# A graph-attention layer on one Trainium2 core: the second round in another order, the pair products as one row, a shared normalise, and a new load order

## The chip, the cores and the metric

The kernel runs on one core of one Trainium2 chip. Five engines work side by side: TensorE (PE, matrix products, weight loads as PEld), VectorE (DVE), ScalarE (ACT), GpSimd (POOL) and SyncE (SP, which here only issues DMAs). Each works through its own list of instructions in order, and waits at semaphores for the others. The metric is the device time of one execution in microseconds, lower is better; the median of several runs counts.

## What is computed

The input x has 128 graphs of 64 nodes with 384 features, and adj is a 128 x 64 x 64 matrix of integer edge types. Cut to what matters, the reference is:

```python
h = jnp.maximum(_layernorm(x, axis=-1), 0.0)
dep_emb = dep_emb_table[adj]
hi_t = einsum('bid,de->bie', h, W1_w[:HID])[:, :, None, :] + einsum('bijd,de->bije', dep_emb, W1_w[HID:]) + W1_b
hj_t = einsum('bjd,de->bje', h, W2_w[:HID])[:, None, :, :] + einsum('bijd,de->bije', dep_emb, W2_w[HID:]) + W2_b
relevance = jnp.sum(hi_t * hj_t, axis=-1)
A = softmax(where(adj != 0, relevance, NEG), axis=2)
h_syn = relu(einsum('bij,bjd->bid', A, h) @ gcn_w + gcn_b)
out = x + h_syn @ Wo_w + Wo_b
```

adj holds only 0 and 1 here, so every edge has the same embedding. With p and q the two projections of that embedding, the relevance becomes h M h^T plus a term per row, a term per column and a constant, with M = W1 W2^T and the "pair products" W2 p, W1 q and p.q.

## The kernel before

The 128 graphs are cut into 16 rounds ("supers", NSUP = 16, LAST = 15) of 8 graphs, that is 512 rows of x, as four tiles (k) of 128 rows. The features are three chunks (c, d) of 128. Every large product is made in float16 with a high and a low part of each operand, three matmuls for one (`split_product`, L1028 to L1030: high x high, high x low, low x high). For each round s:

- **h** is the normalised input. VectorE makes the statistics (L637), POOL makes ln_mul and ln_add in 20 small dependent steps (`coefficients`, L340), ScalarE writes h_tok (float32) and the high half of h_parts (float16) with two passes for each tile (`normalise`, L451), POOL subtracts to get the low half (`token_low`, L402), and a DMA transposes h_parts into one of two buffers hT (L261). Rounds 0 and 1 are transposed by TensorE instead (`early_transposes`, L1073).
- **G = M h^T** in three chunks (`g_chunk`) into PSUM banks 0 to 2. ScalarE writes the high half and a whole copy (L483, L488), VectorE the low half (`g_low_part`, L785).
- **hg = h gcn_w** in four tiles (`hg_tile`) into banks 0, 1, 2 and 0 again, so each tile waits until G's bank has been read (`g_split`). A 385th column is the row term of the scores. ScalarE copies the high half (L502), VectorE the row term and the low half (L908, L712). SP moves the halves into hg_parts by DMA (`move_hg`).
- **scores** (L1106), softmax on VectorE and ScalarE (L915 to L951, L611), attention transposed on TensorE (L1222), copied by ScalarE (L573) and VectorE (`attention_high`, L889), then **aggregation** z = A hg one round later (L1255, L1260), z's halves by ScalarE (`z_parts`, L495, L497) and VectorE (`z_low_part`, L894), and the output product with Wo (`O_BANK`), added to x by VectorE (L902). POOL adds the bias Wo_b to x before (`add_bias`, L408).

The order is written out by hand for each engine. TensorE's round s is: G(s) with the transposed attention of round s-1 inside it, hg tile 0, aggregation of s-1, hg tiles 1 to 3, scores(s), output(s-1). The first two rounds stand apart. The **head** loads W1 and W2, transposes them, makes M and the pair products, makes power-of-two scales for gcn_w and M out of their peaks (`peak_to_row`, `row_top`, `peak_to_all`: column to row on TensorE, maximum on VectorE, one value to all partitions on TensorE), and computes hg(0) (banks 0, 1, 2, 4), G(0) and scores(0). The **second round** is `iteration(1, prev2=False)` of each engine: G(1), hg tiles 0 and 1 with the attention's transpose between them, aggregation, hg tiles 2 and 3, scores, output. A branch on has_types (`typed`, L244) stands before the transposes of round 1; it is taken only for adjacencies with more than one type, and its condition is computed by VectorE (L794, `types_known`).

## Time and profile before

| | |
|---|---|
| median of 3 runs | 378.81 us (375.56 to 379.2) |
| the profiled execution's own time | 379.19 us |
| its span, first to last instruction | 377.3 us |
| mean granted TensorE clock | 0.982 |
| TensorE busy | 358.4 us, 95% |
| TensorE weight loads | 222.8 us, 59% |
| VectorE busy | 268.2 us, 71% |
| ScalarE busy | 273.7 us, 73% |
| GpSimd busy | 178.3 us, 47% |
| share of TensorE in the chain that ended last | 87% |

The profile is one execution. Its timeline gives for every engine the start of an instruction, its length and, in brackets, how long the engine stood idle before it and what released it. The windows view gives for a stretch how long each engine was busy and the mean granted clock of TensorE (1.00 is 2.4 GHz, 0.50 is 1.2 GHz). Matmuls overlap: a row's length is longer than the distance to the next one.

### The profile page before, as it was taken

Reading aid. Unit: us, or ns where it says so; the run is one execution under the profiler, and the core shown is the slowest. Engines: PE = TensorE matmul, PEld = TensorE weight load, DVE = VectorE, ACT = ScalarE, POOL = GpSimd, SP = SyncE. Lnnn points to the kernel's source line nnn. Section 1 sums busy time; section 2 is a strip of 40 time slices with the busy share of each in tenths; the row PEclk is TensorE's granted clock in tenths of the full one; section 3 lists DMA queues with packets and bytes.
Section 4 is the critical chain, followed back from the end, with each engine's and each line's share of the span. In section 5 each row is a group of like instructions: output and inputs, shape, how many; then the busy total and the mean of one; then the engine's idle time right before and its main releaser. Section 6 shows DMA issues by size and latency. Waiting matters only on the chain.

```text
span 377.3 us, 9541 instructions
## 1 busy us (share of the span) xinstructions
PE 358.4 (95%) x3154; PEld 222.8 (59%) x3154; DVE 268.2 (71%) x665; ACT 273.7 (73%) x580; POOL 178.3 (47%) x349
## 2 busy tenths in 40 slices
PE   7899883999999999999999999999999999999986
PEld 6564542656575656656565757566665656575653
DVE  1688878659686877777694958677776859576674
ACT  2375679297969788787879697887878787964733
POOL 2017506647372728274655637282836565490000
PEclk9889998799999999999999999999999999999999
DMA  8972412439564839384654646393937543434043
GB/s 237 287 246 80 108 65 50 119 104 171 151 164 130 203 83 250 84 220 114 187 126 133 156 140 175 97 236 83 250 83 199 135 127 78 132 87 147 19 123 130
DMA packets 82215, 53.87 MB, mean 143 GB/s; under 512 B 45666, under 2 KB 82148, under 8 KB 82196
## 3 DMA queue, kind: packets, MB, share of 16 engines
q1 hardware_dynamic: 81492, 52.64, 51.7%
q10 hardware_dynamic: 640, 0.79, 0.7%
q0 software_dynamic: 64, 0.20, 0.3%
q8 instruction: 11, 0.18, 0.2%
q14 instruction: 8, 0.07, 0.1%
HBM read 17.44 MB, written 12.58 MB: 80 GB/s over the span
## 4 chain that ended last, share of the span: by engine, by line
PE 87%; DVE 5%; ACT 4%; DMA 2%; issue 1%; ACTq 0%; DVEq 0%
PE bank L1028 23%; PE bank L1029 23%; PE bank L1030 23%; PE bank L1106 6%; PE bank L1260 3%; PE bank L1255 3%; PE bank L1080 2%; DMA e_col<-L_gnn_dep_emb_table_dram 2%; PE bank L1222 1%; ACT bank L611 1%; ACT h_parts L451 1%; ACT h_tok L460 1%; PE bank L1323 1%; ACT h_tok L451 1%; PE bank L1325 1%
## 5 line engine op out<-in xcount | busy, mean ns | idle before, releaser
L402 POOL TENSOR_TENSOR h_parts<-h_tok,h_parts 128x1536 f16<-128x1536 f32 x14 | 43.4, 3098 | 99.0 <-ACT h_parts L451 99.0
L1028 PE MATMUL bank<-gw_hi,hT 128*128 128x385 f16 (+2 forms) x204 | 65.2, 324 | 7.6 <-DVE hg_lo L712 6.1
L1030 PE MATMUL bank<-gw_hi,hT 128*128 128x385 f16 (+2 forms) x204 | 64.9, 323 | 0.0
L1029 PE MATMUL bank<-gw_lo,hT 128*128 128x385 f16 (+2 forms) x204 | 64.8, 322 | 0.0
L1028 PE MATMUL bank<-wo_hi,z_hi 128*128 128x384 f16 x180 | 58.7, 326 | 0.0
L1029 PE MATMUL bank<-wo_lo,z_hi 128*128 128x384 f16 x180 | 58.7, 326 | 0.0
L1030 PE MATMUL bank<-wo_hi,z_lo 128*128 128x384 f16 x180 | 58.7, 326 | 0.0
L408 POOL TENSOR_TENSOR x_all<-x_all,bo_all 128x1536 f32 (+1 forms) x16 | 56.2, 3520 | 0.0
L1028 PE MATMUL bank<-hT,m_hi 128*128 128x512 f16 x144 | 54.6, 379 | 0.0
L1030 PE MATMUL bank<-hT,m_lo 128*128 128x512 f16 x144 | 54.6, 379 | 0.0
L1029 PE MATMUL bank<-hT,m_hi 128*128 128x512 f16 x144 | 54.6, 379 | 0.0
L785 DVE TENSOR_TENSOR g_parts<-bank,g_parts 128x512 f16<-128x512 f32 x48 | 33.0, 690 | 23.9 <-ACT bank L488 23.5
L483 ACT ACTIVATE g_parts<-bank,pair_bias 128x512 f16<-128x512 f32 x48 | 32.9, 686 | 15.9 <-PE bank L1030 15.8
L451 ACT ACTIVATE h_tok<-x_all,ln_add,ln_mul 128x384 f32 (+1 forms) x56 | 39.3, 702 | 5.7 <-POOL ln_add L340 5.7
L495 ACT ACTIVATE z_hi<-bank,gcn_bias 128x512 f16<-128x512 f32 x48 | 33.7, 702 | 11.8 <-PE bank L1260 11.8
L502 ACT ACTIVATE hg_hi<-bank 128x384 f16<-128x384 f32 x64 | 32.5, 509 | 13.0 <-PE bank L1030 13.0
L451 ACT ACTIVATE h_parts<-x_all,ln_add,ln_mul 128x384 f16 (+1 forms) x56 | 39.1, 698 | 0.0
L894 DVE TENSOR_TENSOR z_lo<-bank,z_hi 128x512 f16<-128x512 f32 x48 | 32.8, 683 | 8.5 <-ACT bank L497 8.5
L902 DVE SCALAR_TENSOR_TENSOR x_all<-bank,out_scale,x_all 128x384 f32 (+1 forms) x64 | 36.4, 610 | 1.5 <-PE bank L1329 1.1
L712 DVE SCALAR_TENSOR_TENSOR hg_lo<-bank,hg_hi 128x384 f16<-128x384 f32 x64 | 35.0, 550 | 0.2 <-issue 0.2
L497 ACT ACTIVATE bank<-bank,gcn_bias 128x512 f32<-128x512 f32 x48 | 32.6, 678 | 0.0
L1028 PEld LDWEIGHTS bank<-gw_hi,hT 128*128 128x128 f16 x204 | 20.0, 99 | 21.3 <-DVE hg_lo L712 6.5
(149 smaller groups left out, 679.7 us busy)
## 6 DMA issues: line engine op xcount, KB each, us to landing
x_all<-in_x_dram SPq DMA_DIRECT2D x16, 768.0 KB, 6.4
out_dram<-x_all SPq DMA_DIRECT2D x15, 768.0 KB, 4.0
hg_parts<-hg_lo SPq DMA_DIRECT2D x32, 192.0 KB, 3.0
hg_parts<-hg_hi SPq DMA_DIRECT2D x32, 192.0 KB, 3.2
out_dram<-x_all SPq DMA_DIRECT2D x4, 192.0 KB, 1.9
x_all<-in_L_gnn_W_w_dram SPq DMA_DIRECT2D x1, 576.0 KB, 5.5
x_all<-in_L_gnn_W_w_dram ACTq DMA_DIRECT2D x1, 576.0 KB, 6.1
gcn_raw<-in_L_gnn_gcn_w_dram SPq DMA_DIRECT2D x1, 576.0 KB, 10.1
```

The lines of the kernel that those rows point to most:

```text
L402: nc.gpsimd.tensor_tensor(h_parts[:, :, 1, :], h_tok[:, :, :], h_parts[:, :, 0, :], ALU.subtract).then_inc(h_split, 1)
L408: nc.gpsimd.tensor_tensor(x_all[:, s, :, :], x_all[:, s, :, :], bo_all[:, :, :].broadcast_to([P, KT, D]), ALU.add).then_inc(x_biased, 1)
L451: nc.scalar.activation(to, x_all[:, s, k, :], ACT.Relu, bias=ln_add[:, k:k + 1], scale=ln_mul[:, k:k + 1]).then_inc(h_ready, 1)
L483: nc.scalar.activation(g_parts[:, c, :, 0, :], g_bank[c], ACT.Identity, bias=pair_bias[:, c:c + 1], scale=PROJ).then_inc(g_high, 1)
L495: nc.scalar.activation(z_hi[:, c, :], z_bank, ACT.Relu, bias=gcn_bias[:, c:c + 1], scale=Z_DOWN).then_inc(z_high, 1)
L712: nc.vector.scalar_tensor_tensor(hg_lo[:, k, :], bank[hg_banks(s)[k]][:, 0:D], PROJ, hg_hi[:, k, :], ALU.mult, ALU.subtract).then_inc(hg_s ...
L785: nc.vector.tensor_tensor(g_parts[:, c, :, 1, :], g_bank[c], g_parts[:, c, :, 0, :], ALU.subtract).then_inc(g_split, 1)
L894: nc.vector.tensor_tensor(z_lo[:, c, :], z_bank, z_hi[:, c, :], ALU.subtract).then_inc(z_split, 1)
L902: nc.vector.scalar_tensor_tensor(x_all[:, s, k, :], bank[O_BANK[k]][:, 0:D], out_scale[:, 0:1], x_all[:, s, k, :], ALU.mult, ALU.add).then ...
L1028: nc.tensor.matmul(dst, lh, rh, start=(c == 0), stop=False)
L1029: nc.tensor.matmul(dst, lh, rl, start=False, stop=False)
L1030: last = nc.tensor.matmul(dst, ll, rh, start=False, stop=(c == DC - 1))
```

## The change

- **Loads.** W2 is issued by SP behind W1 instead of by ScalarE; ScalarE issues e_col first, then the two small W parts. x(1) no longer waits for x(0) to land, and has a semaphore of its own.
- **Pair products.** W2 p and p.q, twelve products of one column before, become one row: three products with p as the stationary operand (1 x 385), copied by ScalarE, turned back into columns by four one-row products behind hg tile 0.
- **Peaks.** The maxima of |M|, |pairs| and |Wo| on VectorE become sums of |.| on ScalarE (`m_norm`, `wo_norm`).
- **Head order.** VectorE normalises all four tiles of round 0 (two before), makes statistics(1) before the low parts, M's vector low part earlier and g_low(0, 1) after has_types. ScalarE normalises round 1 before the copies of G(0). POOL makes the coefficients of round 1 before the first mask. A few products on `ones` (`keep_warm`) stand behind the W1 transposes and the e_col products.
- **Second round.** hg(1) stands ahead of G(1), in banks 0, 1, 2, 4, and hg(0) has a buffer pair of its own (`hg_pair`), so that hg(1)'s halves can be written before aggregation(0) has read hg(0)'s. All four tiles of hg(1) come before G(1); aggregation, scores and output follow.
- **Normalise of round 2** is shared: ScalarE (and POOL for the low half) makes tiles 0 and 1, VectorE tiles 2 and 3 with six instructions (`shared_normalise`). ScalarE's normalise(3) stands undivided behind exponentials(1), and VectorE's statistics(3) behind the last z_low(0).

```diff
+        first_hg_hi, first_hg_lo = (x_all[:, NSUP - 4 + n, 0:2, :].bitcast(f16).rearrange("p a b -> p (a b)")
+                                    .rearrange("p (k d) -> p k d", k=KT) for n in range(2))
...
-            return FIRST_HG_BANK if isinstance(s, int) and s == 0 else HG_BANK
+            return EARLY_HG_BANK if isinstance(s, int) and s < 2 else HG_BANK
+        def hg_pair(s):
+            return (first_hg_hi, first_hg_lo) if isinstance(s, int) and s == 0 else (hg_hi, hg_lo)
...
                 sp.wait_ge(h_split, s - 1)
+                if s == 2:
+                    sp.wait_ge(h_shared, KT - ACT_TILES)
...
             sp.dma_start(w1_raw, W1[0:D, :].rearrange("(c p) e -> p c e", p=P)).then_inc(w1_loaded, 16)
+            sp.dma_start(w2_raw, W2[0:D, :].rearrange("(c p) e -> p c e", p=P)).then_inc(w2_loaded, 16)
...
-            sp.wait_ge(x_loaded, 16)
             load_x(1)
...
+            main_coefficients(1)
             make_bias(0)
-            main_coefficients(1)
             make_bias(1)
...
+                tiles = slice(0, ACT_TILES) if isinstance(s, int) and s == 2 else slice(0, KT)
+                nc.gpsimd.tensor_tensor(h_parts[:, tiles, 1, :], h_tok[:, tiles, :], h_parts[:, tiles, 0, :],
                                         ALU.subtract).then_inc(h_split, 1)
...
+            m_copy(0)
             gcn_norm()
-            m_copy(0)
+            m_norm(0)
             m_copy(1)
-            early_normalise(0, range(EARLY_WIDE, KT))
+            m_norm(1)
             m_copy(2)
+            m_norm(2)
+            act.wait_ge(pair_row_done, 1)
+            nc.scalar.activation(pair_row[:, :], bank[7][0:1, 0:D + 1], ACT.Copy).then_inc(pair_row_copied, 1)
+            act.wait_ge(pair_row_copied, 1)
+            act.wait_ge(m_norms, DC)
+            nc.scalar.activation(norm_scratch[0:1, 0, 0:D], pair_row[:, 0:D], ACT.Abs,
+                                 accum_out=peak_part[0:1, DC:DC + 1]).then_inc(m_norms, 1)
             for c in range(DC):
                 gcn_high_part(c)
                 early_high_part(0, c)
...
             types_excess(0)
+            hg_high_part(0, 0)
             types_excess(1)
-            hg_high_part(0, 0)
             hg_high_part(0, 1)
+            wo_norm()
...
+            nc.scalar.activation(gw_hi[:, :, D], pair_vec[:, 1, :], ACT.Copy,
+                                 scale=scale[:, SC_M:SC_M + 1]).then_inc(gw_high, 1)
             for k in range(2, KT):
                 hg_high_part(0, k)
-            nc.scalar.activation(gw_hi[:, :, D], pair_vec[:, 1, :], ACT.Copy,
-                                 scale=scale[:, SC_M:SC_M + 1]).then_inc(gw_high, 1)
+            early_normalise(1, range(KT))
             for c in range(DC):
-                if c == DC - 1:
-                    early_normalise(1, range(KT))
                 g_high_part(0, c)
                 g_whole(c)
...
+            def second_round():
+                move_scores(0)
+                hg_high_part(1, 0)
+                normalise(2, range(0, 1))
+                hg_high_part(1, 1)
+                exponentials(0)
+                hg_high_part(1, 2)
+                normalise(2, range(1, ACT_TILES))
+                hg_high_part(1, 3)
+                g_high_part(1, 0)
+                g_whole(0)
+                act.wait_ge(wo_scale_ready, 1)
+                nc.scalar.activation(wo_hi[:, :, :], wo_raw[:, :, :], ACT.Copy,
+                                     scale=scale[:, SC_WO:SC_WO + 1]).then_inc(wo_high, 1)
+                g_high_part(1, 1)
+                attention_out(1)
+                g_whole(1)
+                g_high_part(1, 2)
+                g_whole(2)
+                for c in range(DC):
+                    z_parts(0, c, bank[Z_BANK[c]][:, :])
+                move_scores(1)
+                exponentials(1)
+                normalise(3)
...
-            for k in range(EARLY_WIDE):
+            for k in range(KT):
...
-            for d in range(2):
-                dve.wait_ge(m_copied, d + 1)
-                magnitude(d, m_raw[:, d, :], AX.X, m_peaks)
+            statistics(1)
             for c in range(DC):
                 gcn_low_part(c)
                 early_low_part(0, c)
-            dve.wait_ge(m_copied, 3)
-            magnitude(2, m_raw[:, 2, :], AX.X, m_peaks)
+            dve.wait_ge(m_norms, DC + 1)
+            nc.vector.tensor_reduce(peak_row[:, :], peak_part[:, 0:DC + 1], AX.X, ALU.max).then_inc(m_peaks, 1)
...
+            hg_low_part(0, 1)
+            dve.wait_ge(gw_high, DC + 1)
+            low_part(gw_lo[:, :, D], pair_vec[:, 1, :], gw_hi[:, :, D], SC_M).then_inc(gw_vector, 1)
...
             g_low_part(0, 0)
-            dve.wait_ge(gw_high, DC + 1)
-            low_part(gw_lo[:, :, D], pair_vec[:, 1, :], gw_hi[:, :, D], SC_M).then_inc(gw_vector, 1)
-            g_low_part(0, 1)
             row_top(TYPE_TOP, bank[6][0:1, TYPE_ROW], type_row, top_read)
             dve.wait_ge(top_read, 4)
             nc.vector.tensor_scalar(has_types[0:1, :], peak_one[0:1, TYPE_TOP:TYPE_TOP + 1], 0.0, None,
                                     ALU.is_gt).then_inc(types_known, 1)
             statistics(2)
+            g_low_part(0, 1)
             g_low_part(0, 2)
...
+                rows_and_low(1, 0)
+                rows_and_low(1, 1)
+                row_top(WO_TOP, bank[WO_BANK][0:1, WO_ROW], wo_row, wo_top)
                 attention(0, prev=False)
+                rows_and_low(1, 2)
+                output_scale()
+                rows_and_low(1, 3)
+                shared_normalise(2)
+                g_low_part(1, 0)
+                g_low_part(1, 1)
+                attention_high(1, prev2=False)
+                dve.wait_ge(wo_high, 1)
+                low_part(wo_lo[:, :, :], wo_raw[:, :, :], wo_hi[:, :, :], SC_WO).then_inc(wo_split, 1)
+                g_low_part(1, 2)
+                for c in range(DC):
+                    z_low_part(0, c, bank[Z_BANK[c]][:, :])
+                statistics(3)
+                masked_scores(1)
+                add_output(0, range(2))
+                attention(1)
+                add_output(0, range(2, KT))
+            def shared_normalise(s):
+                dve.wait_ge(coef_ready, COEF_STEPS * (s + 1))
+                nc.vector.tensor_tensor(first["sum"], stats6[:, :, 1], stats6[:, :, 4], ALU.add).then_inc(coef_step, 1)
+                dve.wait_ge(coef_step, 17)
+                nc.vector.tensor_scalar(first["gap"], first["sum"], 0.5, None, ALU.mult).then_inc(coef_step, 1)
+                dve.wait_ge(coef_step, 18)
+                dve.wait_ge(early_t, 2)
+                for k in range(ACT_TILES, KT):
+                    mean = first["gap"][:, k:k + 1]
+                    nc.vector.tensor_scalar(h_tok[:, k, :], x_all[:, s, k, :], mean, mean,
+                                            ALU.max, ALU.subtract).then_inc(coef_step, 1)
+                for k in range(ACT_TILES, KT):
+                    dve.wait_ge(coef_step, 19 + k - ACT_TILES)
+                    nc.vector.tensor_scalar(h_parts[:, k, 0, :], h_tok[:, k, :], ln_mul[:, k:k + 1], None,
+                                            ALU.mult).then_inc(coef_step, 1)
+                for k in range(ACT_TILES, KT):
+                    dve.wait_ge(coef_step, 19 + k - ACT_TILES + KT - ACT_TILES)
+                    nc.vector.scalar_tensor_tensor(h_parts[:, k, 1, :], h_tok[:, k, :], ln_mul[:, k:k + 1],
+                                                   h_parts[:, k, 0, :], ALU.mult, ALU.subtract).then_inc(h_shared, 1)
...
+                if n == 0:
+                    keep_warm(KEEP_WARM)
...
+            for c in range(DC):
+                last = nc.tensor.matmul(bank[7][0:1, 0:D + 1], p_col[:, c:c + 1], w2T[:, c, :],
+                                        start=(c == 0), stop=(c == DC - 1))
+            last.then_inc(pair_row_done, 1)
             early_transposes(0)
-            for e in range(DC):
-                for c in range(DC):
-                    nc.tensor.matmul(bank[7][:, e:e + 1], w2T[:, c, e * P:(e + 1) * P], p_col[:, c:c + 1],
-                                     start=(c == 0), stop=(c == DC - 1))
-            pe.wait_ge(q_copied, 3)
-            for c in range(DC):
-                last = nc.tensor.matmul(bank[7][:, PAIR_PQ:PAIR_PQ + 1], ones[:, :], pq_part[:, c:c + 1],
-                                        start=(c == 0), stop=(c == DC - 1))
-            last.then_inc(pairs_done, 1)
...
+                    pe.wait_ge(m_peaks, 1)
+                    pe.wait_ge(pair_row_copied, 1)
                     peak_to_row(bank[7][0:1, ROW], peak_row[:, :], m_row)
+                    for c in range(DC):
+                        nc.tensor.matmul(bank[6][:, c:c + 1], pair_row[0:1, c * P:(c + 1) * P], ones[0:1, 0:1],
+                                         start=True, stop=True)
+                    nc.tensor.matmul(bank[6][:, PAIR_PQ:PAIR_PQ + 1], ones[0:1, :], pair_row[0:1, D:D + 1],
+                                     start=True, stop=True).then_inc(pairs_done, 1)
...
+            def second_round():
+                for k in range(KT):
+                    hg_tile(1, k, 1)
+                    if k == 1:
+                        pe.wait_ge(score_copied, GT)
+                        pe.wait_ge(summed, GT)
+                        pe.wait_ge(wo_peak, 1)
+                        peak_to_row(bank[WO_BANK][0:1, WO_ROW], peak_part[:, DC + 1:DC + 2], wo_row)
+                    if k == 2:
+                        peak_to_all(bank[WO_BANK][:, WO_WIDE:WO_WIDE + 1], WO_TOP, wo_top, wo_wide)
+                for c in range(DC):
+                    hg_read(KT + c + 1)
+                    g_chunk(c, 1)
+                    if c == 1:
+                        transposed_attention(1)
+                aggregation(1, Z_BANK)
+                pe.wait_ge(g_split, DC * 2)
+                pe.wait_ge(wo_scale_ready, 1)
+                scores_of(1, 1)
+                pe.wait_ge(wo_split, 1)
+                output(1)```

VectorE, the second round of the kernel before, from the exponential's bias of round 0 (exp_bias) to the first low part of z (z_lo); L685 is the peak of Wo, L785 are the low parts of G(1), L889 the high part of the transposed attention, L705 the low part of Wo:

```order
L934 TENSOR_SCALAR exp_bias<-row_max,exp_nscale 128x4
L685 TENSOR_REDUCE peak_part<-x_all 128x1
L939 RECIPROCAL row_inv<-row_sum 128x4
...
L785 TENSOR_TENSOR g_parts<-bank,g_parts 128x8x64 x3
L889 COPY attT_hi<-bank 64x4x64 x2
...
L637 BN_STATS stats<-x_all 128x6 x4
L705 SCALAR_TENSOR_TENSOR wo_lo<-x_all,scale,wo_hi 128x1152
L894 TENSOR_TENSOR z_lo<-bank,z_hi 128x512
L908 TENSOR_SCALAR row_term<-bank,pq_scaled 128x1
L712 SCALAR_TENSOR_TENSOR hg_lo<-bank,hg_hi 128x384
```

The same stretch of VectorE in the changed kernel, from the fourth low part of hg(1); L1042 to L1057 are the shared normalise, L840 the low parts of G(1), L942 the attention's high part, L765 Wo's low part:

```order
L773 SCALAR_TENSOR_TENSOR hg_lo<-bank,hg_hi 128x384
L1042 TENSOR_TENSOR first_sum<-stats 128x4
L1044 TENSOR_SCALAR first_gap<-first_sum 128x4
L1049 TENSOR_SCALAR h_tok<-x_all,first_gap 128x384 x2
L1053 TENSOR_SCALAR h_parts<-h_tok,ln_mul 128x384 x2
L1057 SCALAR_TENSOR_TENSOR h_parts<-h_tok,ln_mul,h_parts 128x384 x2
L840 TENSOR_TENSOR g_parts<-bank,g_parts 128x8x64 x2
L942 COPY attT_hi<-bank 64x4x64 x2
L765 SCALAR_TENSOR_TENSOR wo_lo<-x_all,scale,wo_hi 128x1152
L840 TENSOR_TENSOR g_parts<-bank,g_parts 128x8x64
L947 TENSOR_TENSOR z_lo<-bank,z_hi 128x512 x3
L697 BN_STATS stats<-x_all 128x6 x4
```

The hg low parts moved ahead of the attention and of G(1), the shared normalise is new, and the statistics of round 3 moved from ahead of Wo's low part to behind the three z low parts.

TensorE in the head of the changed kernel, from M (L1169) to the first hg product (L1111); L1140 turns a column of peaks into a row, L1145 gives one value to all partitions, L1178 is the pair row, L1162 are the transposes of round 0:

```order
L1169 MATMUL bank<-x_all 128x385 x6
L1140 MATMUL bank<-ident,peak_part 1x128
L1169 MATMUL bank<-x_all 128x385 x3
L1145 MATMUL bank<-peak_one,ones 128x1
L1178 MATMUL bank<-x_all,p_col 1x385 x3
L1162 MATMUL bank<-ident,h_tok 128x128 x12
L1111 MATMUL bank<-gw_hi,hT 128x384
```

And in the kernel before, the same stretch (L1080 is M, L1073 the transposes, L1091 and L1095 the pair products):

```order
L1080 MATMUL bank<-x_all 128x385 x3
L1057 MATMUL bank<-peak_one,ones 128x1
L1073 MATMUL bank<-ident,h_tok 128x128 x12
L1091 MATMUL bank<-p_col,x_all 128x1 x9
L1095 MATMUL bank<-pq_part,ones 128x1 x3
L1028 MATMUL bank<-gw_hi,hT 128x384
```

The pair products moved from behind the transposes to ahead of them, as three wide products.

## Rows read from the trace of the kernel before

**Rows 1.** TensorE's waits, first 100 us: engine, line, releaser, total, times, longest

```profile
PE bank L1028 <- DVE hg_lo L712: 6.1, 1, 6.1
PE bank L1064 <- DMA e_col<-L_gnn_dep_emb_table_dram: 1.8, 1, 1.8
PE bank L1073 <- ACT h_tok L460: 1.6, 1, 1.6
...
PE bank L1028 <- DVE g_parts L785: 1.2, 1, 1.2
```

**Rows 2.** TensorE's waits from 75 us to the end

```profile
PE bank L1255 <- DVE attT_hi L889: 1.3, 1, 1.3
```

**Rows 3.** TensorE's timeline: start, length in us, engine, line, out<-in, count

```profile
17.89 2.11 PE L1080 MATMUL bank<-x_all 128*128 128x385 f32 x6
...
41.44 1.53 PE L1073 MATMUL bank<-ident,h_tok 128*128 128x128 f32 x12 [1.63 <-ACT h_tok L460]
...
76.51 0.38 PE L1028 MATMUL bank<-hT,m_hi 128*128 128x512 f16 x1
...
82.64 0.33 PE L1028 MATMUL bank<-gw_hi,hT 128*128 128x385 f16 x1
```

**Rows 4.** Windows: stretch, length, busy PE, PEld, DVE, ACT, POOL, clock, DMA

```profile
12.20:15.50 3.30, 3.30 (x6) 1.78 (x7) 2.87 (x17) 1.26 (x2) 0.00 (x0) 0.50 0.86 276
...
25.90:29.10 3.20, 3.20 (x11) 1.29 (x10) 2.78 (x11) 1.43 (x3) 2.02 (x2) 0.50 0.32 54
...
40.00:43.70 3.70, 2.26 (x48) 2.25 (x49) 2.54 (x7) 2.44 (x6) 1.20 (x7) 1.00 0.31 77
```

**Rows 5.** VectorE's timeline, head to round 2

```profile
16.07 0.87 DVE L724 TENSOR_SCALAR h_tok<-x_all,ln_mul,ln_add 128x384 f32<-128x384 f32 x2
...
39.87 0.14 DVE L794 TENSOR_SCALAR has_types<-peak_one 1x1 int32<-1x1 f32 x1
...
48.47 0.23 DVE L934 TENSOR_SCALAR exp_bias<-row_max,exp_nscale 128x4 f32<-128x4 f32 x1
...
57.69 1.93 DVE L637 BATCH_NORM_STATS2 stats<-x_all 128x6 f32<-128x384 f32 x4
61.11 3.20 DVE L705 SCALAR_TENSOR_TENSOR wo_lo<-x_all,scale,wo_hi 128x1152 f16<-128x1152 f32 x1 [1.49 <-ACT wo_hi L587]
...
64.95 0.54 DVE L712 SCALAR_TENSOR_TENSOR hg_lo<-bank,hg_hi 128x384 f16<-128x384 f32 x1
...
81.52 0.69 DVE L785 TENSOR_TENSOR g_parts<-bank,g_parts 128x512 f16<-128x512 f32 x1 [0.89 <-ACT bank L488]
```

**Rows 6.** ScalarE's timeline, head to round 2

```profile
21.43 0.61 ACT L469 ACTIVATE gw_hi<-gcn_raw,scale 128x384 f16<-128x384 f32 x1 [0.90 <-DVE gcn_bias L734]
...
48.73 0.38 ACT L611 ACTIVATE bank<-bank,exp_bias,exp_scale 128x64 f32<-128x64 f32 x1
...
50.28 0.69 ACT L483 ACTIVATE g_parts<-bank,pair_bias 128x512 f16<-128x512 f32 x1
...
60.97 0.67 ACT L495 ACTIVATE z_hi<-bank,gcn_bias 128x512 f16<-128x512 f32 x1
...
62.11 0.48 ACT L502 ACTIVATE hg_hi<-bank 128x384 f16<-128x384 f32 x1
...
73.95 0.71 ACT L451 ACTIVATE h_tok<-x_all,ln_add,ln_mul 128x384 f32<-128x384 f32 x1 [2.25 <-POOL ln_add L340]
...
80.27 0.68 ACT L483 ACTIVATE g_parts<-bank,pair_bias 128x512 f16<-128x512 f32 x1
```

**Rows 7.** POOL's timeline in the second round and behind it

```profile
60.00 3.09 POOL L402 TENSOR_TENSOR h_parts<-h_tok,h_parts 128x1536 f16<-128x1536 f32 x1 [11.66 <-ACT h_parts L451]
...
67.55 0.20 POOL L340 TENSOR_TENSOR root_sq<-stats 128x4 f32<-128x4 f32 x1
...
73.71 0.20 POOL L340 TENSOR_TENSOR ln_add<-root_sq,const_all 128x4 f32<-128x4 f32 x1
...
83.52 3.45 POOL L408 TENSOR_TENSOR x_all<-x_all,bo_all 128x1536 f32 x1
```

300 lines of the change are left out of this document (144 added, 156 removed).

## The prediction

> **What bounds the kernel now.** I read the waits of TensorE first. In the first 100 us it waits for four things that matter: 6.1 us for the low part of hg(0) in the second round, 1.8 for the DMA of e_col, 1.6 for the normalised tokens of round 1, 1.2 for G(1) [rows 1]. After 75 us it waits once more for over 1 us [rows 2]: from round 2 on the time is TensorE's own work, and nothing there is changed. So the question is one number: how much sooner does the steady part begin? I take hg tile 0 of round 2, which starts at 82.64 in the timeline of TensorE, 6.13 after G(2) at 76.51 [rows 3]; everything behind it follows back to back. The windows show why the waits cost more than their length: at 12.2 to 15.5 and 25.9 to 29.1 the granted clock is 0.50 (1.2 GHz), both times behind a stretch in which TensorE idled or ran products of one column; over 40.0 to 43.7, with 1.4 us idle in it, it stays at 1.00 [rows 4].
>
> **The head, up to the known types.** w2 now follows w1 on SP and e_col comes first on ScalarE's queue, so the six e_col products need not wait 1.8 us [rows 1], and M starts some 2 us sooner, near 10.1. At full clock three of its nine products take 2.0 (2.11 with the last one's tail [rows 3]), so it ends near 16.4, with a short wait for the norm of gcn_w in it. That is not gained: the gcn scale needs VectorE, and VectorE needs x(0). Its h_tok begins at 16.07 and costs 0.87 for two tiles [rows 5], now four: 17.8. The row maximum behind it ends at 18.1, TensorE broadcasts by 18.5, makes the pair row (three products of 385 columns, 1.95, in the place of twelve of one column) by 20.5, and ScalarE, which stands at the pair row's copy, takes 0.5 and a norm of 0.6 before it scales gcn_w: 21.6, against 21.43 [rows 6]. So the whole new load order is hidden behind x(0); I put the head at 0 until the first hg products. The four one-row products behind hg tile 0 cost TensorE about 0.8; statistics(1) is out of the way of the M scale, but the M scale waits for TensorE (hg tile 1), as before.
>
> From there VectorE's order decides has_types. Before it is at 39.87 [rows 5]. Now a g_low (0.69 [rows 5]) and the low part of M's vector no longer stand between the adjacency maximum and it; the low part now stands ahead of the maximum, and ScalarE's wo_norm delays m_hi by some 0.35. I take 39.1. The round 1 transposes, at 41.44 before [rows 3], wait for the branch on it: 40.8, **0.6 sooner**. From them to the exponential's bias it took 48.47 + 0.23 - 41.44 = 7.3 [rows 3, 5]; nothing in between is changed: 48.1.
>
> **The second round.** TensorE runs hg(1) at once, in banks that nobody holds, and G(1) behind it: 44.8 to 57.6 with 0.5 idle. The old 6.1 and 1.2 us [rows 1] are gone. What is late next is VectorE and ScalarE:
> - POOL's 20 coefficient steps take 6.3 (67.55 to 73.91) [rows 7]; for round 2 they start at 41.1 (statistics 1.94 behind has_types) and end at 47.4. ScalarE then does a half share of normalise(2), a tile being two passes of 0.6 (eight and the exponentials lie between 73.95 and 80.27), hg copies of 0.4 to 0.5, and exponentials(0) of 1.55 (48.73 to 50.28) [rows 6]: 50.7, 52.3 with the second tile.
> - VectorE: two hg low parts (0.54 and a short row term each) [rows 5], attention(0) 1.6 to 52.3, a third low part 52.9, output_scale 1.15 to 54.05, the fourth 54.65. Then shared_normalise: 0.4, two passes of 0.43 over two tiles 1.75, to 56.8, and two low parts of 0.53.
> - POOL meanwhile: its low part of two tiles, half of 3.09, to 53.9, and add_bias(0) of 3.45 [rows 7], to 57.3. The old trace shows what this does: wo_lo, which reads two SBUF tiles, took 3.20 [rows 5] while POOL's low part ran from 60.00 to 63.09 [rows 7]; it ended 1.2 behind POOL's end. So the two low parts of shared_normalise wait from 56.8 to 57.3 and end at 58.4. The Trainium skill, "SBUF — State Buffer", section "Who interferes with whom", says the same: a VectorE instruction with two SBUF inputs and a GpSimd one that reads SBUF exclude each other for the whole instruction. It adds that tensor_scalar can do so too, which is a rival below.
> - Two g_low of 0.62 and attention_high 0.6: 60.2. TensorE, done at 57.6, waits 2.6 and aggregates from 60.3.
>
> **The third round's tokens.** z(0,0) is done at 60.8. ScalarE's three z pairs cost 1.14 each (60.97 to 62.11) [rows 6], to 64.2; VectorE's last z_low ends at 65.0 and output(1) can run from 65.0 to 70.9. G(2) would start at 70.9 instead of 76.51: 5.6 sooner. But statistics(3), which was at 57.69 before [rows 5], now stands behind z_low(0,2): 1.93, 65.0 to 66.9. POOL's 6.3 give the coefficients at 73.25, where they came at 73.91 [rows 7]: only 0.65 sooner. Normalise(3), eight passes of 0.6, runs then without exponentials in it (they lay inside 73.95 to 80.27 before [rows 6]) and ends at 78.1. G(2)'s first high and whole copies are behind it on ScalarE, 1.25, and VectorE's g_low(2,0), 0.69, was at 81.52 [rows 5]: now 79.4 to 80.05. TensorE, which reaches hg tile 0 at 70.9 + 6.13 = 77.0, waits 3.0 us there.
>
> **Sum.** Hg tile 0 of round 2 at 80.05 instead of 82.64: 2.6 us. Taken from the profiled execution's own 379.19 (span 377.3 and 1.9 around it) that is 376.6; the median before is 378.81 of three from 375.56 to 379.2, so the profiled one is a common one. The new wait of 3 us has a price of its own where the clock falls behind it: 3.3 us at 1.2 GHz cost 1.65, as at 12.2 to 15.5 [rows 4]. The 40.0 to 43.7 stretch kept the clock over 1.4 us idle, the thin stretch before 25.9 did not. 3.0 lies between. I take a small part of it, 0.2, and forecast **376.8**. Bounds of the unseen: the shared passes (0.43 each by h_tok's 0.87 for two, 0.54 at most, the length of a low part [rows 5]) 0 to +0.5; the branch's share 0 to -0.6; x(0) landing 0.5 either way, which moves all; the clock fall 0 to +1.65 at each of two places. The likeliest case spans 375.2 to 378.4.
>
> **Rivals.**
> - *TensorE gets through without the 3 us wait.* If attention_high came 2 us sooner (VectorE pairs overlapping better than my sum of single rows) and POOL's steps took less than 6.3, the steady part would start up to 5.6 sooner: 373.6. Against it: 20 dependent steps that took 6.3 in every round. 18%.
> - *The exclusion takes the tensor_scalar passes too.* Then all six of shared_normalise wait for add_bias's end at 57.3 and end at 60.2, 1.8 later; aggregation, statistics(3) and hg tile 0 follow: 81.85, gain 0.8: 378.4. No row of this trace shows a tensor_scalar beside a long POOL instruction, so the case stays open on the rows. 17%. (It is the Trainium skill's rule for tensor_scalar in its two-port modes, same page and section.)
> - *The clock makes it slower.* New idle stretches of TensorE lie at 16.4 to 18.2 (for x(0)), 57.6 to 60.3 and 77.0 to 80.05. If the clock falls behind the first, the pair row and the transposes take 1.9 longer, all on the path; behind the second, aggregation 0.5; behind the third 1.65: together 4.0 against a gain of 2.6, 380.6, slower than before. It decides from 2.6 us of lost clock on. For it: the clock of 25.9 to 29.1 fell behind thin work that had no long gap in it [rows 4]. 15%.
> - *The gain stops at hT(2):* its transpose is late and nothing behind it moves, 379.2. Its low parts end at 58.4 instead of 63.09 [rows 7], so the transpose is early. 2%.
> The likeliest case keeps 48%.
>
> **Numbers.** Range 373.3 to 380.4: it takes in the first three cases and most of the clock's. Over 1% (3.8 us, about what a measurement of this kernel can tell from no change) faster, below 375.0, takes 0.15 of the first rival's 0.18 and 0.13 of the likeliest case's 0.48, where x(0) lands early or the clock does not fall at 25.9: 0.28. Within 1%: 0.64. Slower by over 1%, above 382.6, needs the second and third rivals together: 0.08.
>
> **What would show it.** hg(1) straight behind scores(0) near 45, with no wait for G(1). A wait of TensorE at the aggregation of about 2.6 on attT_hi near 60, and one of about 3 on g_parts near 77 to 80. has_types near 39.1. POOL's last step for round 3 near 73.2, started by stats near 66.9. VectorE's two low parts of shared_normalise ending just behind POOL's add_bias. I am wrong in the head if M's scale comes before 30.5 or after 32, and wrong in the sum if G(2)'s first chunk stands with less than 1 us between its end and hg tile 0.

## The result, and the profile after

The changed kernel is slower. In its own comparison it took 384.19 us (median of 4 executions, 382.08 to 386.85) against 378.98 for the kernel before: ratio 1.0156, 95% interval 1.0079 to 1.0234. Run again beside the experiments (after_again, for which I had expected 383 to 385) it took 381.79 us (12 executions, 379.48 to 383.26) against 378.25: ratio 1.0070, interval 1.0046 to 1.0094. The forecast was 376.8, range 373.3 to 380.4: wrong in sign and outside the range.

| | before | after | after, run again |
|---|---|---|---|
| the profiled execution's own time, us | 379.19 | 386.85 | 381.74 |
| its span | 377.3 | 385.0 | 379.9 |
| mean granted TensorE clock | 0.982 | 0.969 | 0.987 |
| exp_bias of round 0 starts | 48.47 | 53.98 | 49.16 |
| from there to exp_bias of round 2 | 45.8 | 47.2 | 47.0 |
| from there to the end | 283.0 | 283.8 | 283.8 |
| TensorE / VectorE / ScalarE busy | 358.4 / 268.2 / 273.7 | 365.0 / 269.0 / 273.8 | |

From round 3 to round 13 every round lasts 20.6 us in both kernels. Most of the difference is made in the first 100 us. The waits of TensorE there, in the changed kernel's first profile (who waited for whom, us in total, times, longest), to be held against [rows 1]:

```profile
PE bank L1342 <- DVE attT_hi L942: 3.9, 1, 3.9
PE bank L1111 <- DVE g_parts L840: 3.0, 1, 3.0
PE bank L1111 <- DVE hT L703: 2.0, 2, 1.6
PE bank L1152 <- DMA x_all<-in_L_gnn_W_b_dram: 2.0, 1, 2.0
PE bank L1145 <- DVE peak_one L742: 1.3, 1, 1.3
```

The 6.1 us for hg_lo are gone, as forecast. 3.9 us for the attention and 3.0 for G(2) stand in their place (forecast 2.6 and 3.0), with 1.3 for the maximum of Wo's peaks (L1145, at 56.3), which was not forecast, and the wait ahead of the edge embedding's products (L1152), which was to vanish, has only changed its cause: 2.0 us, now for a bias row. TensorE's timeline of the head, same profile (start, length, engine, line, operation, [idle before, released by]), against [rows 3]:

```profile
10.25 2.16 PE L1152 MATMUL bank<-e_col,x_all 65*128 65x1 f32 x12 [1.99 <-DMA x_all<-in_L_gnn_W_b_dram]
...
19.48 2.11 PE L1169 MATMUL bank<-x_all 128*128 128x385 f32 x6
21.52 0.38 PE L1145 MATMUL bank<-peak_one,ones 1*128 1x1 f32 x2
21.82 2.10 PE L1178 MATMUL bank<-x_all,p_col 128*1 128x385 f32 x6
23.86 1.53 PE L1162 MATMUL bank<-ident,h_tok 128*128 128x128 f32 x12
26.95 0.32 PE L1111 MATMUL bank<-gw_hi,hT 128*128 128x384 f16 x1 [1.56 <-DVE hT L703]
```

The pair row (L1178) runs ahead of the early transposes (L1162), and TensorE idles 1.56 us behind them. The windows of the same profile (stretch, length, busy of PE, PEld, DVE, ACT, POOL, then granted clock, DMA share, GB/s), against [rows 4]:

```profile
10.90:17.70 6.80, 6.80 (x19) 4.72 (x19) 5.19 (x23) 0.58 (x3) 0.00 (x0) 0.50 0.96 311
28.00:38.00 10.00, 9.96 (x34) 5.20 (x35) 3.53 (x15) 5.45 (x12) 4.76 (x15) 0.50 0.18 66
40.00:68.00 28.00, 22.50 (x195) 12.68 (x192) 24.51 (x62) 19.63 (x40) 11.85 (x23) 1.00 0.22 60
69.00:72.30 3.30, 3.30 (x59) 3.21 (x57) 2.49 (x4) 3.30 (x6) 0.00 (x0) 0.50 0.79 181
```

At 0.50, the 1.2 GHz level, TensorE spent 17 us of the head here, in five stretches of 3.4; before it was two. In the second round the row that costs most has four elements. VectorE's and GpSimd's timelines, same profile:

```profile
60.69 2.89 DVE L1042 TENSOR_TENSOR first_sum<-stats 128x4 f32<-128x4 f32 x1
63.62 0.17 DVE L1044 TENSOR_SCALAR first_gap<-first_sum 128x4 f32<-128x4 f32 x1
63.82 0.87 DVE L1049 TENSOR_SCALAR h_tok<-x_all,first_gap 128x384 f32<-128x384 f32 x2
...
67.52 0.59 DVE L942 COPY attT_hi<-bank 64x256 f16<-64x256 f16 x2
68.14 1.42 DVE L765 SCALAR_TENSOR_TENSOR wo_lo<-x_all,scale,wo_hi 128x1152 f16<-128x1152 f32 x1
...
73.03 1.93 DVE L697 BATCH_NORM_STATS2 stats<-x_all 128x6 f32<-128x384 f32 x4
```
```profile
60.12 3.44 POOL L421 TENSOR_TENSOR x_all<-x_all,bo_all 128x1536 f32<-128x1536 f32 x1
75.03 0.30 POOL L349 TENSOR_TENSOR root_sq<-stats 128x4 f32<-128x4 f32 x1 [11.47 <-DVE stats L697]
```

The sum of the means takes 2.89 us where it takes 0.16 alone, and ends with GpSimd's add_bias (63.58 and 63.56).

### The profile page after: what moved, and what is told of

Its sections match the earlier page's. It is cut to its first block, busy times and chain, and to the rows that moved or that the text cites. A ratio compares the mean times of both kernels' runs of the same rounds, so it can differ in the third digit from the quotient of the medians.

```text
span 385.0 us, 9525 instructions
## 1 busy us (share of the span) xinstructions
PE 365.0 (95%) x3152; PEld 226.1 (59%) x3152; DVE 269.0 (70%) x669; ACT 273.8 (71%) x585; POOL 177.1 (46%) x350
## 4 chain that ended last, share of the span: by engine, by line
PE 80%; DVE 7%; ACT 5%; POOL 3%; DMA 2%; issue 2%; SPq 0%; DVEq 0%; ACTq 0%; POOLq 0%
PE bank L1111 21%; PE bank L1112 21%; PE bank L1113 21%; PE bank L1190 5%; PE bank L1347 3%; PE bank L1342 3%; DMA x_all<-in_L_gnn_W_b_dram 2%; PE bank L1169 2%; POOL root_sq L349 1%; DVE stats L697 1%; PE bank L1311 1%; ACT bank L626 1%; POOL root L349 1%; DVE first_sum L1042 1%; ACT h_parts L463 1%
## 5 line engine op out<-in xcount | busy, mean ns | idle before, releaser
L415 POOL TENSOR_TENSOR h_parts<-h_tok,h_parts 128x1536 f16<-128x1536 f32 (+1 forms) x14 | 41.9, 2994 | 91.4 <-ACT h_parts L463 91.4
L1111 PE MATMUL bank<-gw_hi,hT 128*128 128x385 f16 (+2 forms) x204 | 65.6, 326 | 5.0 <-DVE g_parts L840 3.0
L1111 PE MATMUL bank<-wo_hi,z_hi 128*128 128x384 f16 x180 | 58.7, 326 | 0.5 <-DVE z_lo L947 0.5
L421 POOL TENSOR_TENSOR x_all<-x_all,bo_all 128x1536 f32 (+1 forms) x16 | 55.0, 3443 | 0.0
L1111 PE MATMUL bank<-hT,m_hi 128*128 128x512 f16 x144 | 54.6, 379 | 0.0
L840 DVE TENSOR_TENSOR g_parts<-bank,g_parts 128x512 f16<-128x512 f32 x48 | 33.0, 691 | 28.5 <-ACT bank L501 28.1
L496 ACT ACTIVATE g_parts<-bank,pair_bias 128x512 f16<-128x512 f32 x48 | 32.8, 684 | 15.6 <-PE bank L1113 15.5
L463 ACT ACTIVATE h_tok<-x_all,ln_add,ln_mul 128x384 f32 (+1 forms) x54 | 37.9, 702 | 7.1 <-POOL ln_add L349 6.9
L947 DVE TENSOR_TENSOR z_lo<-bank,z_hi 128x512 f16<-128x512 f32 x48 | 32.9, 685 | 10.0 <-ACT bank L510 10.0
L463 ACT ACTIVATE h_parts<-x_all,ln_add,ln_mul 128x384 f16 (+1 forms) x54 | 37.7, 698 | 0.0
L515 ACT ACTIVATE hg_hi<-bank 128x384 f16<-128x384 f32 x60 | 30.6, 510 | 8.5 <-PE bank L1113 8.0
L773 DVE SCALAR_TENSOR_TENSOR hg_lo<-bank,hg_hi 128x384 f16<-128x384 f32 x60 | 32.9, 548 | 0.0
L697 DVE BATCH_NORM_STATS2 stats<-x_all 128x6 f32 (+1 forms) x64 | 30.9, 546 | 2.7 <-DMA x_all<-in_x_dram 2.7
```

The source lines that it names most:

```text
L415: nc.gpsimd.tensor_tensor(h_parts[:, tiles, 1, :], h_tok[:, tiles, :], h_parts[:, tiles, 0, :], ALU.subtract).then_inc(h_split, 1)
L421: nc.gpsimd.tensor_tensor(x_all[:, s, :, :], x_all[:, s, :, :], bo_all[:, :, :].broadcast_to([P, KT, D]), ALU.add).then_inc(x_biased, 1)
L463: nc.scalar.activation(to, x_all[:, s, k, :], ACT.Relu, bias=ln_add[:, k:k + 1], scale=ln_mul[:, k:k + 1]).then_inc(h_ready, KT // ACT_TIL ...
L697: ins = nc.vector.bn_stats(stats6[:, k, :], x_all[:, s, k, :])
L773: nc.vector.scalar_tensor_tensor(low[:, k, :], bank[hg_banks(s)[k]][:, 0:D], PROJ, high[:, k, :], ALU.mult, ALU.subtract).then_inc(hg_spli ...
L840: nc.vector.tensor_tensor(g_parts[:, c, :, 1, :], g_bank[c], g_parts[:, c, :, 0, :], ALU.subtract).then_inc(g_split, 1)
```

## The clock first: how much of it is chance

Executions of one and the same kernel differ in how often the clock falls. In all the profiles the low clock of the first 100 us comes in pieces of 3.4 us, and the mean granted clock of an execution counts them: 0.991, 0.987, 0.982, 0.978, 0.973, 0.969 for two to seven. The executions by that number (mean us, how many; the kernel before without its first four, and without two at 0.995 with 376.1):

| clock | 0.99 | 0.985-0.987 | 0.980-0.982 | 0.977-0.978 | 0.973 | 0.969 |
|---|---|---|---|---|---|---|
| before | 376.7 (8) | 377.9 (42) | 379.2 (60) | 380.7 (2) | | |
| after | 380.4 (5) | 381.9 (5) | 382.8 (3) | 383.2 (1) | 385.2 (1) | 386.9 (1) |

One low stretch costs some 1.2 us. At an equal clock, where both have three executions or more, the changed kernel is 3.6 to 4.0 us slower. The first four executions of it had 3, 5, 6 and 7 such stretches, the next twelve 2 to 4 (before mostly 3 and 4): that is why its two comparisons differ by 1.7 us. So the clock makes the first result look worse, but it is not the whole cause. The comparison has a limit: where a kernel's own waits make the clock fall or keep it up, the number of low stretches is part of its effect, and comparing at equal clock takes that part away. The rest of the document looks for the 3.8 us.

## Experiments

All medians beside the kernel before on the same chip; "+2.6" is the difference to it.

**1. Old head, new second round (old_head).** Undoes the change up to scores(0), but for the peak of Wo, which stays on ScalarE.

> The head of the kernel before (its load order, M's pairs as four columns, gcn's peak ahead of M's copy, no extra warming products, early transposes where they stood) with the second round of the changed kernel. Theory, the head: the changed kernel reached its first aggregated products 5 us late (exp_bias ended at 53.98 instead of 48.47) and its second round gained nothing. Then exp_bias ends at 48.5 +- 0.5, the distance from there to hg tile 0 of round 2 is 34.3 as in the changed kernel, and the whole is within 1% of before: 379 +- 2. Rival, the second round: its new order (the wait of 3.9 us for the second round's attention, the clock that falls behind it) costs the time and the head is made good somewhere; then this kernel stays at 383 or more although exp_bias is at 48.5.

381.23, +2.6 (ratio 1.0065, 1.0042 to 1.0087). exp_bias at 47.89 as expected, but 47.8 us from there to round 2's (45.8 before), with the same four low stretches in the profile, one of them behind the 3.0 us wait for G(2). At 0.986 its executions took 379.8 (3) against 377.9, at 0.982 381.8 (5) against 379.2. Both theories hold a half: the second round costs some 2 us by itself, the head the rest, 1 to 2 us.

**2. The sum of the means earlier (sum_early).** The two instructions leave shared_normalise; their semaphores are left out here.

```diff
             g_low_part(0, 2)
+            nc.vector.tensor_tensor(first["sum"], stats6[:, :, 1], stats6[:, :, 4], ALU.add)
+            nc.vector.tensor_scalar(first["gap"], first["sum"], 0.5, None, ALU.mult)
```

> The changed kernel with one thing moved: the sum and the half sum of the means (two VectorE instructions on 128x4 elements, 2.89 us and 0.17 us in the changed kernel) run at about 50 us, behind g_low(0,2), and no longer beside GpSimd's add_bias. Theory, only an instruction of VectorE that reads two SBUF tensors waits for GpSimd: the h_tok and h_parts passes, which read one tensor and a scalar column, start at 60.7 instead of 63.8, attention_high of round 1 ends 2 to 3 us sooner, TensorE's wait there falls from 3.87 to about 1, and the whole falls by 2 to 3 us against the changed kernel: 381 to 382 where that gives 384. Rival, GpSimd's tensor_tensor holds up every pass over SBUF: then the first h_tok pass takes some 3 us, nothing comes earlier, and the time is that of the changed kernel, 384 (+5 us over before). Second rival: the passes come earlier, but wo_lo or statistics(3) takes the gain, and hg tile 0 of round 2 starts where it did from exp_bias (34.3 us later).

382.41, +3.8: nothing won. The first pass over x now waits in its stead; this row of VectorE by line gives minimum, median and maximum in ns:

```profile
L1050 DVE TENSOR_SCALAR h_tok<-x_all,first_gap x2: 469/1778/3086, 54.9 to 57.9; 128x384 f32<-128x384 f32 x2
```

The first of the two passes took the 3.09 us from 54.9; add_bias ran from 54.35 to 57.79. So tensor_scalar passes over SBUF wait as well, which was the second rival of the forecast (17%).

**3. add_bias earlier (bias_ahead), and held until exp_bias is written (after_wait).** The line with wait_ge is in after_wait alone.

```diff
             main_coefficients(2)
-            iteration(1)
+            pool.wait_ge(exp_bias_ready, 1)
+            add_bias(0)
+            token_low(2)
+            main_coefficients(3)
```

> The changed kernel with GpSimd's add_bias(0) ahead of the low parts of the tokens of block 2: it runs for 3.44 us in the 4.9 us that GpSimd waited there, beside VectorE's passes over PSUM, and is over when VectorE's sum of the means and its h_tok pass come. Theory, GpSimd's add_bias holds up every VectorE pass that works from SBUF (the sum took 2.89 us; with the sum moved away the first h_tok pass took 3.09 instead of 0.47): the sum takes 0.16, h_tok 0.5 each, attention_high of round 1 ends 2.7 us sooner after exp_bias (10.8 us instead of 13.5), TensorE's wait for it falls from 3.9 to about 1.1, and the whole to 2 to 2.7 us below the changed kernel of this call, a median of 381.5. Rival, the stall only moves: masked scores, reciprocal or the low parts of the first tiles wait for add_bias in its new place, exp_bias of round 0 or the attention of round 0 comes 2 us later, and nothing is won. Second rival: the wait falls, but the wait of 3.0 us for g_low(2,0) grows by as much, since normalise(3) stays late: hg tile 0 of round 2 starts 34.3 us after exp_bias as it did.

> The changed kernel with add_bias(0) ahead of the tokens' low parts on GpSimd, held by one more wait until exp_bias of round 0 is written. In the run with add_bias earlier but without that wait, exp_bias (128x4 elements, 0.23 us otherwise) took 2.63 us beside add_bias: the stall had moved to where it holds up ScalarE's exponentials. Theory: between exp_bias and the sum of the means VectorE runs passes over PSUM, 128x1 passes and a reciprocal, none of which was long beside a GpSimd pass in any of these traces; so no VectorE instruction waits for add_bias now, exp_bias takes 0.2, the sum 0.2, attention_high of round 1 ends 10.8 us after exp_bias instead of 13.5, and the whole is 1.5 to 2.7 us below the changed kernel (+3.5 us over before in 12 runs): +1 to +2. Rival: the reciprocal (128x4) or the 128x1 passes are held up as well, and nothing is won. Second rival: the wait turns up again at g_low(2,0), behind normalise(3), and half or less arrives.

bias_ahead: 383.38, +5.1 (at 0.987 382.4 of three, the changed kernel 381.9). The stall moved to a place where ScalarE's exponentials wait for it. GpSimd, then VectorE:

```profile
46.89 3.44 POOL L421 TENSOR_TENSOR x_all<-x_all,bo_all 128x1536 f32<-128x1536 f32 x1
```
```profile
47.73 2.63 DVE L989 TENSOR_SCALAR exp_bias<-row_max,exp_nscale 128x4 f32<-128x4 f32 x1
```

after_wait: the same rows with one more wait.

```profile
48.17 3.44 POOL L421 TENSOR_TENSOR x_all<-x_all,bo_all 128x1536 f32<-128x1536 f32 x1 [1.10 <-DVE exp_bias L990]
```
```profile
47.87 0.23 DVE L990 TENSOR_SCALAR exp_bias<-row_max,exp_nscale 128x4 f32<-128x4 f32 x1
49.09 0.55 DVE L776 SCALAR_TENSOR_TENSOR hg_lo<-bank,hg_hi 128x384 f16<-128x384 f32 x1
50.49 0.18 DVE L995 RECIPROCAL row_inv<-row_sum 128x4 f32<-128x4 f32 x1 [0.67 <-ACT bank L629]
54.28 0.16 DVE L1045 TENSOR_TENSOR first_sum<-stats 128x4 f32<-128x4 f32 x1
58.48 0.59 DVE L945 COPY attT_hi<-bank 64x256 f16<-64x256 f16 x2
```

Nothing waits for add_bias any more, and the attention's copy ends 11.2 us behind exp_bias instead of 14.1. The median, 381.65 (+3.2), hardly shows it: at 0.991 four executions took 378.3 (380.4 for the changed kernel), but five of the other eight had five low stretches and 382.8. The 3.0 us wait for G(2) was still there. So the stall behind add_bias costs the changed kernel about 2 us at equal clock. That the median hides it lies in the number of low stretches (a mean of 3.7, 2.8 in the changed kernel); whether this is chance or comes with the step, no run shows.

**4. Both repairs, and statistics(3) earlier (pair_fix, old_head_fix, old_head_best).** pair_fix (with the head of pair_norm, 6 below) and old_head_fix (with the old head) take bias_ahead and put statistics(3) behind attention_high of round 1. old_head_best takes the held add_bias and this order:

```diff
                 attention_high(1, prev2=False)
+                g_low_part(1, 2)
+                statistics(3)
                 dve.wait_ge(wo_high, 1)
                 low_part(wo_lo[:, :, :], wo_raw[:, :, :], wo_hi[:, :, :], SC_WO).then_inc(wo_split, 1)
-                g_low_part(1, 2)
                 for c in range(DC):
                     z_low_part(0, c, bank[Z_BANK[c]][:, :])
-                statistics(3)
```

> The changed kernel with the pair row behind the early transposes and gcn's peak ahead of M's copy (alone: 380.8, +2.1 us over before), and two things in its second round: add_bias(0) ahead of the tokens' low parts on GpSimd, and statistics(3) right behind attention_high of round 1, ahead of wo_lo. Theory: 2.7 us from the first, as in the run beside it, and 1.9 us from the second (ScalarE waited 1.93 us for GpSimd's coefficients at normalise(3); TensorE's wait of 2.8 us for g_low(2,0) falls to about 1), together 4.5 us off 380.8: 376.5, 2 us faster than before. From exp_bias of round 0 to that of round 2: 41.5 instead of 45.7. Rival: GpSimd's coefficients or ScalarE's own queue (exponentials of round 1) are later than I take them for, wo_lo becomes late for the output of round 1, and only half is won: 378.5, no change from before.

> The head of the kernel before with the second round of the changed one (alone: 381.2, +2.6 us over before), and the same two repairs of the second round: add_bias(0) earlier on GpSimd, statistics(3) earlier on VectorE. Theory: 4.5 us off 381.2: 376.7, 2 us faster than before, exp_bias at 47.9 and 41.5 to 43 us from there to that of round 2 (47.8 without the repairs, with one low stretch of the clock there). Rival: the second round of the kernel before was bound by work and not by waits; then the waits vanish and TensorE's clock falls as often, and it stays at 379 or above.

> The head of the kernel before, the second round of the changed one, with add_bias(0) as in the run beside it, and VectorE's order behind attention_high of round 1 as g_low(1,2), statistics(3), wo_lo. With statistics(3) first and add_bias unheld it gave 377.2 (1.1 us faster than before) although exp_bias took 3.28 us and TensorE waited 2.3 us for g_low(1,2), which came behind statistics(3) and wo_lo. Theory: both go, 3 to 5 us: 373.5, 4.5 us faster than before; from exp_bias of round 0 to that of round 2 it is 39 to 40.5 us instead of 45.8 before. Rival: with TensorE's waits gone the round is bound by TensorE itself and by ScalarE's passes, or the clock falls elsewhere: 376 or more.

pair_fix 379.25 (+1.0), old_head_fix 377.19 (-1.1, ratio 0.9962, 0.9933 to 0.9991), both with exp_bias held up for 2.61 and 3.28 us by add_bias, and with TensorE waiting 2.3 us for g_low(1,2). old_head_best: 375.74, **-2.7** (ratio 0.9933, 0.9906 to 0.9961), 40.9 us from exp_bias of round 0 to that of round 2. The gain is smaller than expected (373.5), since one wait takes the place of the others; TensorE's waits in its profile:

```profile
PE bank L1108 <- DVE z_lo L944: 2.9, 1, 2.9
PE bank L1149 <- DMA e_col<-L_gnn_dep_emb_table_dram: 1.8, 1, 1.8
PE bank L1159 <- ACT h_tok L478: 1.6, 1, 1.6
PE bank L1339 <- DVE attT_hi L939: 1.2, 1, 1.2
```

Of the 2.7 us some 1.2 are there at equal clock (376.6 of six executions at 0.985 to 0.986, 377.8 for twelve of the kernel before beside them); the rest is fewer low stretches, a mean of 2.3 against 3.3. The profiles show where they went, the kernel before first, old_head_best below:

```profile
63.40:70.20 6.80, 4.65 (x42) 3.11 (x43) 5.48 (x15) 2.74 (x6) 6.33 (x8) 0.50 0.51 116
```
```profile
55.00:90.00 35.00, 30.84 (x316) 19.51 (x315) 28.06 (x66) 27.23 (x55) 17.32 (x42) 1.00 0.52 135
```

The two low stretches of the kernel before lie around its wait of 6.1 us, which is gone. So part of the lower count may well be the new order's own; one profile of each does not prove it.

**5. The repair in the kernel before (before_wait).** The held add_bias, nothing else.

> The kernel before with one thing changed: add_bias(0) runs right behind exp_bias of round 0 and ahead of the low parts of block 2, in the 11.7 us that GpSimd idled there. It tells what the repair brings without the second round's new order. Theory: GpSimd's coefficients of block 3 start at 63.1 instead of 67.6, normalise(3) waits for them 0 instead of 2.25 us, the wait of 1.2 us for g_low(2,0) goes, wo_lo stays at 3.20 (it waits for the low parts of the tokens), the 6.1 us wait for hg_lo stays: 1.2 us faster, 377. Rival, the new order of the second round is worth nothing and the repairs all: then this gives as much as the best of the changed ones, 374. Second rival: nothing at all, since normalise(3) is not on the path: 378.3.

378.49, +0.0 (0.9982 to 1.0029), with the waits of 6.1 and 1.3 us where they were. So the held add_bias gives nothing without the new order of the second round, and the new order without the repairs costs time (old_head). The other repair, statistics(3) ahead of wo_lo, was not run in the kernel before.

**6. The head: its order (pair_norm, pair_late).** pair_late puts TensorE's pair row behind early_transposes(0) and ScalarE's copy and norm of it behind the high parts; pair_norm also puts gcn_norm() back ahead of m_copy(0).

> The changed kernel with two things of its head put back in place: TensorE's three products of M's pair row stand behind the early transposes, with ScalarE's copy and norm of the row behind the high parts of the gcn weight and the first tile; and ScalarE takes gcn's peak ahead of M's first copy. Theory, the order of the head: gw_hi, at 25.0 us in the changed kernel and 21.4 before, comes at 22 to 22.5 (the 2.1 us of the pair row with its weights and the 1.0 us of ScalarE's wait leave the chain), the M scale (peak at 35.9) comes 1.5 to 3 us sooner, exp_bias ends at 51 +- 0.7 instead of 54, and the whole falls by 2.5 to 3.5 us against the changed kernel, to 381 (+2 us over before). Rival, the clock and the loads: the early transposes are late because M's own products ran at 1.2 GHz and the columns of the edge embedding came late; then gw_hi moves by less than 1 us and the whole stays within 1 us of the changed kernel, +5 us over before.

> The changed kernel with TensorE's pair row behind the early transposes and ScalarE's copy and norm of it behind the high parts, but gcn's peak behind M's first copy as in the changed kernel. At the same clock the run with both moves brought gw_hi 1.7 us sooner (20.3 instead of 22.0) but exp_bias not at all (48.1 against 47.7 to 48.5), for the 2.1 us of the pair row then stand ahead of hg tile 0 and M's peak waits for them. Theory, TensorE's products in the head are a sum that no order shortens: exp_bias at 47.7 to 48.5 with no low stretch in the head, 49 with one, the whole as the changed kernel, +3 to +3.5, unless the clock falls less often. Rival: M's peak, now with no wait of ScalarE for the pair row, comes sooner and the whole falls to +2, as in the run with both moves; then the mean granted clock would be the same as the changed kernel's at a shorter time.

pair_norm 380.77 (+2.1), pair_late 381.96 (+3.0). The first looked like a success, but its five executions at 0.99 took 380.3, the changed kernel's 380.4; eight of pair_late's nine had 0.985 to 0.987 and 382.0, against 381.9. Its gain was fewer low stretches. In pair_late gw_hi came 2.3 us sooner (21.18 against 23.44 in the profile with the same low stretch in the head), exp_bias 0.2 sooner (49.00, 49.16). Two things took it: the pair row now stands between the transposes and hg tile 0, and VectorE's pair_bias, 0.27 us in the changed kernel, met GpSimd's first mask, with which it ends (GpSimd, then VectorE):

```profile
30.36 1.90 POOL L395 TENSOR_SCALAR adj_all<-adj_all 128x2048 f32<-128x2048 int32 x1
```
```profile
30.27 0.15 DVE L751 TENSOR_SCALAR peak_bits<-peak 128x1 int32<-128x1 int32 x1
30.71 0.15 DVE L759 TENSOR_SCALAR scale<-flip_bits 128x1 f32<-128x1 f32 x1
30.90 1.38 DVE L813 TENSOR_SCALAR pair_bias<-pair_vec,scale 128x3 f32<-128x3 f32 x1
```

**7. That mask earlier (mask_first, pair_best_mask).** make_bias(0) ahead of main_coefficients(1) on GpSimd, in pair_late and in pair_best (below).

> The run with the pair row behind the early transposes, and GpSimd's make_bias(0) ahead of its coefficients of block 1, as in the kernel before. With the coefficients first, make_bias(0), a pass of 1.90 us over 128x2048 elements, ran from 30.36 to 32.26, and VectorE's pair_bias (128x3, 0.27 us in the changed kernel) took 1.38 us, ending with it, so that m_hi started 2.23 us behind M's peak instead of 1.1 to 1.2. Theory: moving the pair row does free 1.1 us, and this collision takes it back. With make_bias(0) at about 26.5 pair_bias takes 0.3, m_hi starts 1.1 us behind M's peak, exp_bias of round 0 comes 1.0 to 1.1 us sooner than in that run at the same clock (48.0 with one low stretch), and the whole is 0.9 to 1.1 us below it: 380.9, +2 over before. Rival: the round's own start, which waits for TensorE and the types, is not bound by m_hi, and nothing moves: 382.

> The run with all repairs, and make_bias(0) ahead of the coefficients of block 1 as well. It gave 376.2 with exp_bias at 49.4 (one low stretch) and m_hi 2.23 us behind M's peak. Theory: 1.1 us less, 375.1, 3.5 us faster than before, level with or better than the old head beside the repaired second round (375.7). Rival: the 1.1 us come back as a wait of TensorE for z_low (2.9 us in both repaired second rounds) or are lost to the clock: 376.2.

mask_first 385.14 (+6.0), pair_best_mask 380.34 (+1.2): worse. The step itself came as expected (pair_bias 0.23, m_hi 1.0 us sooner), but make_bias(0) waits for both of ScalarE's counts of types and ran at 28.84, so the 20 coefficient steps behind it ended at 37.7, and ScalarE has early_normalise(1) ahead of G(0)'s copies:

```profile
37.74 2.50 ACT L472 ACTIVATE h_tok<-x_all,ln_add,ln_mul 128x384 f32<-128x384 f32 x4 [3.86 <-issue]
```

G(0)'s first copy (40.14) follows 3.0 us later than in pair_late, has_types (42.3) and the transposes (43.86) 2.6, and the clock is low for three stretches from 42.2 on.

**8. Loads, warming products, the norm of Wo (loads_back, bias_first, no_keep, wo_moved).** loads_back restores the load order. bias_first issues the two bias rows ahead of W2. no_keep sets KEEP_WARM to 0. wo_moved puts wo_norm() ahead of hg_high_part(0, 1).

> The changed kernel with the loads issued as before (W2 on ScalarE's queue behind W1, the edge embedding behind it, x(1) once x(0) has landed). Theory: the loads cost little; x(0) lands 0.9 us sooner (statistics(0) started at 11.84 instead of 10.94), TensorE's wait at 10.25 for the bias rows turns into the old one for the edge column and keeps its length, and the whole is 0 to 1 us below the changed kernel (+4 to +5 us over before). Rival, the loads set the head: x(0) and the bias rows late by 1 us or more pull the low clock of 10.9 to 17.7 us in; with the old order the low clock begins at 12.1 and lasts 3.4 us, M's products end 1.5 us sooner and exp_bias follows at 52 instead of 54, the whole 2 us or more below the changed kernel.

> The changed kernel with the two bias rows issued ahead of W2 on SP's queue. In the prediction the edge embedding's products no longer waited, since their column was loaded first on ScalarE's queue; in all profiles of the changed kernel they still wait 1.0 to 2.0 us, now for a row of W_b. Theory, these small rows stand behind 590 KB of W2: ahead of it they land 1 us or more sooner, the products start at 9.0 or before instead of 10.0, M's products as much sooner, and the M scale with them as far as statistics(0) and x(0), which lands later by the time of nothing, allow: exp_bias 0 to 1 us sooner, the whole 0 to 1 below the changed kernel. Rival: the wait is for W2 itself or its transposed copies, the start stays at 9.8 to 10.2 and nothing moves.

> The changed kernel without its four extra warming products (two behind a transposed block of W2, two behind the wide product), which run at 0.1 to 0.6 us each while M's operands are awaited. Theory: they are on the path of M's products for up to 1.2 us and keep no clock up: the changed kernel's clock fell at 12.3 or 10.9 us with them in most of its profiles, as in the kernel before without them. The whole is 0 to 1 us below the changed kernel, and the mean granted clock of its executions is as there, 0.982 to 0.991. Rival: they do keep TensorE busy enough that the clock falls less often in the head: without them the mean granted clock goes down by 0.004 to 0.009 (one to two more low stretches of 3.4 us) and the time up by 1.3 to 2.6 us.

> The changed kernel with ScalarE's norm of Wo (1.16 us and its 0.19) ahead of its copy of hg(0,1) instead of behind it. In the changed kernel it stands between that copy and m_hi: m_hi starts 1.2 us behind M's peak instead of 1.1 us behind it where ScalarE is free, that is 2.25 us after the DVE row of the peak in one order and 1.1 in the other. Theory: the norm fits into the 1.04 us in which ScalarE waits for TensorE's hg tile 1, m_hi starts 0.9 to 1.1 us sooner after M's peak, G(0) too, exp_bias of round 0 by 0.5 to 1 (at the same clock), and the whole is 0.5 to 1 us below the changed kernel: +2.5 to +3 over before. Rival: M's scale itself comes only then, ScalarE's queue was free anyway, and nothing moves: +3.5.

- loads_back 382.62 (+4.0): the loads are not it. x(0) lands sooner (statistics at 11.01), the edge products start at 9.65, and at equal clock nothing arrives at the end (382.3 and 382.8 at 0.982).
- bias_first 387.03 (+8.1), against both theories: now W2 itself is late. TensorE waits 2.8 us for it and the edge products start at 12.77; the clock is low from 10.6 to 20.8. Why W2 lands later behind two small rows is not shown.
- no_keep 383.37 (+4.9): at equal clock 0.4 to 0.9 less than the changed kernel (381.5 against 381.9 at 0.987, 381.9 against 382.8 at 0.982), but a mean of 4.7 low stretches against 2.8 in the 12 executions of the changed kernel. That fits the rival, that the few warming products keep the clock up, but does not show it: the first four executions of the changed kernel, with these products, had a mean of 5.3, the two sets ran on different chips, and after_wait, beside no_keep and with the products, had 3.7.
- wo_moved 381.77 (+2.8): at equal clock nothing (380.7, 381.7, 382.4). My premise was wrong: in the changed kernel m_hi starts 1.22 us behind M's peak, not 2.25.

**9. All together with the new head (pair_best).**

> The changed kernel with all repairs: pair row behind the early transposes, gcn's peak first, the norm of Wo ahead of the copy of hg(0,1), add_bias(0) behind exp_bias of round 0, and g_low(1,2), statistics(3), wo_lo in this order behind attention_high of round 1. Beside the head of the kernel before these last two gave 375.7 (2.7 us faster than before). Theory: the head of the changed kernel costs 2 us at the same clock, of which the norm of Wo gives 1 back: 376.7, 1.5 to 2 us faster than before; exp_bias at 47.0 (no low stretch) to 48.0 (one), 40.9 from there to that of round 2. Rival: the head is now free of what held it and equals that of before: 375.7 or less.

376.20, **-2.7** (ratio 0.9929, 0.9899 to 0.9959), level with old_head_best. exp_bias was at 49.42 in the profile where old_head_best has 46.95, so the head still costs some 2.5 us with the same one stretch; fewer low stretches (a mean of 2.0 against 2.3) and the spread of both hide that in the medians. Against the kernel before at equal clock the gain is not settled: 376.2 (6) at 0.989 to 0.991 against 377.8 (3) beside it and 376.7 in the table above, and one execution at 0.986 with 378.1 against 377.8.

**What the new head costs at one low stretch.** TensorE's timelines of before_wait, which has the head of the kernel before, and of the changed kernel run again; in both the clock falls once, from about 12.5 to 16:

```profile
11.75 5.82 PE L1084 MATMUL bank<-x_all 128*128 128x385 f32 x12 [0.42 <-ACT p_col L532]
19.86 1.53 PE L1077 MATMUL bank<-ident,h_tok 128*128 128x128 f32 x12
21.23 2.07 PE L1095 MATMUL bank<-p_col,x_all 128*128 128x1 f32 x18
23.15 0.81 PE L1099 MATMUL bank<-pq_part,ones 128*128 128x1 f32 x6
23.82 0.32 PE L1032 MATMUL bank<-gw_hi,hT 128*128 128x384 f16 x1
39.81 1.53 PE L1077 MATMUL bank<-ident,h_tok 128*128 128x128 f32 x12 [1.63 <-ACT h_tok L464]
```
```profile
12.15 5.82 PE L1169 MATMUL bank<-x_all 128*128 128x385 f32 x12
20.26 2.10 PE L1178 MATMUL bank<-x_all,p_col 128*1 128x385 f32 x6
22.30 1.53 PE L1162 MATMUL bank<-ident,h_tok 128*128 128x128 f32 x12
25.40 0.32 PE L1111 MATMUL bank<-gw_hi,hT 128*128 128x384 f16 x1 [1.57 <-DVE hT L703]
28.30 0.82 PE L1224 MATMUL bank<-ones,pair_row 1*128 1x1 f32 x6
41.44 1.53 PE L1162 MATMUL bank<-ident,h_tok 128*128 128x128 f32 x12 [0.15 <-issue]
```

The old pair products (2.9 us, L1095 and L1099) stood behind the transposes and filled the time in which gcn_w and hT were made. The new row takes 2.1 ahead of them, nothing fills the wait, and the four one-row products take another 1.1 ahead of hg tile 1. hg tile 0 starts 1.6 later, M's peak (28.43, 31.27) and G(0) 2.8 later. The transposes win back 1.2, since they no longer wait for ScalarE's tokens. exp_bias then comes 2.3 later (46.84, 49.16). This split is read from the two timelines. No run puts the twelve small products back and leaves the rest of the new head, so how much of the 2.3 us is the row's own stays open.

## Why the prediction was wrong, step by step

- **The head at 0 until the first hg products: this step failed**, by 1.6 us at hg tile 0 and 2.8 at G(0). The prediction began M near 10.1 and ended it near 16.4, so that the pair row fitted into the wait for x(0). M began at 12.15, as before (12.13), since the bias rows, issued by SP behind W2, landed no sooner than the old e_col: the wait of 1.8 us in [rows 1] had a second cause behind it. It also took M at full clock, though [rows 4] has 12.2 to 15.5 at 0.50: M took 7.9 us instead of 6.3 (6.2 in sum_early, where the clock did not fall there). With M's last third ending at 20, nothing hides the pair row; in sum_early it ended at 18.1 and hg tile 0 still started at 23.96, so the late start is the larger part. The loads would not have saved it (loads_back, bias_first).
- **has_types at 39.1**: 39.84 and 45.02. **Transposes at 40.8**: 41.44 and 46.58. M's scale was to come between 30.5 and 32; it came at 31.90 in the second profile and at 36.49 in the first (M's peak at 31.27 and 35.85). The 0.6 us of gain from this part were not there: with one low stretch in the head the old order has the transposes at 39.81 (before_wait). "Nothing in between is changed" was wrong too: from the transposes to the start of exp_bias it took 7.7 us, 7.0 before. The low part of G(0)'s last chunk now ends behind the transposes (43.28), and VectorE stood idle for 1.05 us between it and its hT passes, which start at 44.33 (43.63 before); what holds them is not shown.
- **The second round: -2.0 us forecast from exp_bias to hg tile 0 of round 2, 0 measured** (34.2 before, 34.3 after). hg(1) ran at once (45.28 in the second profile). The exclusion of VectorE and GpSimd was foreseen, but for the two low parts alone, as a wait of 0.5 us. This is the second step that failed: the exclusion held the first instruction of shared_normalise, the four-element sum, for 2.7, and with it everything behind. The attention's copy ended 13.9 us behind the end of exp_bias instead of 12.1. The rival that priced this at +1.8, with 17%, was the true case of the second round, and after_wait, without the stall, is some 2 us faster at equal clock. It was left at that since "no row shows a tensor_scalar beside a long POOL instruction"; the sum, though, is a tensor_tensor with two SBUF inputs, the kind for which the row on wo_lo [rows 5] did show it. The Trainium skill, "SBUF — State Buffer", section "Who interferes with whom", has both kinds, two inputs in SBUF and tensor_scalar in its two-port modes, and the traces agree: 2.89 for the sum, 3.09 for h_tok, 2.63 and 3.28 for exp_bias, 1.38 for pair_bias, each ending with the GpSimd pass. It says that tensor_scalar contends only when its operands meet the conditions of the mode; that 128x1 passes (0.15) beside the mask were not held is compatible with that, but no run here tests the condition.
- **Two new waits of TensorE, 2.6 and 3.0**: 3.9 and 3.0. Mechanism right, the first 1.3 short. POOL's last coefficient came 27.3 us behind the end of exp_bias instead of 25.1. A third, 1.3 us for the maximum of Wo's peaks at 56.3, was not foreseen but for the 0.5 of idle time in hg(1) and G(1).
- **The clock, +0.2**: the rival at 4.0 was half right. In the second and third round the clock was low for two stretches, as before, but once for each wait, at 63.8 and 84.3. What differs between the profiles is the head, where it is low for 0 (sum_early) to 5 stretches (the first profile). The prediction had one profile; the spread over executions (379.5 to 386.9 for the changed kernel, 375.5 to 381.1 for before) was not in the range.
- **Sum**: with one low stretch in the head, +2.3 up to exp_bias, +1.2 from there to exp_bias of round 2 (all behind hg tile 0, where the clock is low for the second time), and 0.7 behind, of which 0.3 lie in the next round (20.57 us against 20.30) and 0.4 behind the last exp_bias (16.3 against 15.9; before_wait has 16.3 too, so this is not the change): 4.2 in the profiles, 3.6 to 4.0 in the means. Forecast -0.6, -2.0, 0.
- **The chance of a loss**: by the prediction's own terms the second and third rival together give 382.4, still under the 382.6 from which it counts "slower by over 1%", and their chances multiply to 0.03, not 0.08. No rival priced the head.

## What to carry to other kernels

Before an instruction is moved to VectorE, list what GpSimd runs at that moment: any VectorE pass that works from SBUF, down to four elements, may wait out the whole GpSimd pass, and moving the GpSimd pass only moves the wait unless a semaphore lets it go behind the last small instruction that matters. A product that fills a wait is free where it stands; made cheaper (2.9 to 2.1 us) and moved ahead of the transposes, it left a wait of 1.6 us open, and the next tile started 1.6 us later. And when the clock differs from one execution to the next, look at equal granted clock before a gain or a loss is believed: pair_norm's 1.4 us against the changed kernel were none, and of the 2.7 us of old_head_best 1.2 are left.

## What was unexpected of the hardware

- A 128x4 tensor_tensor took 2.89 us instead of 0.16, a 128x4 tensor_scalar 3.28 instead of 0.23. A 128x4 reciprocal (0.18), passes that read PSUM (0.55) and 128x1 passes (0.15) beside GpSimd passes were not held.
- The same program had 2 to 7 low stretches of TensorE's clock in 16 executions, at some 1.2 us each, although a stretch of 3.4 us at half the clock would cost 1.7 of pure TensorE work.
- The mean number of low stretches of one and the same kernel was 5.3 in its first four executions and 2.8 in the next twelve. Beside that, the 4.7 of the kernel without its four products on `ones` (1.3 us together) proves nothing about them.
- Two rows of 1.5 KB ahead of a load of 576 KB made the whole kernel 5 us slower than behind it (387.03 and 381.79 beside 378.94 and 378.25 of the kernel before), with a mean of 6.3 low stretches of the clock against 2.8.
